# Moving the output weights' low half and the ternary weights to GpSimd, with new opening and closing order lists

## The chip, the cores and the metric

The kernel runs on one core of a Trainium2 chip. The metric is the device time of one execution, in microseconds (us). The core has a matrix engine (TensorE, PE), a vector engine (VectorE, DVE), an activation engine (ScalarE, ACT), a general engine (GpSimd, POOL) and a queue that issues transfers (SyncE, SP). Each runs its own instruction list in order and waits for the others through semaphores.

## The reference, cut to what matters

Gated cross attention over a context, then a quantised feed-forward block with ternary weights. There are 32 batches of 112 queries and 375 context rows, model width 256, 16 heads of 64.

```python
# x (32,112,256), ctx (32,375,256); weights in f32
q = layernorm(layernorm(x)) @ Wq ; k, v = split(layernorm(ctx) @ Wkv)
q = (q * (1 + scale) + shift) ; attn = softmax(q k^T / 8) ; out = (attn v) @ Wout
x = x + tanh(g_xattn) * out
def bitlinear(x, w, b):                     # w: one of 3 values times a scale
    scale = 1.0 / clip(mean(abs(w)), 1e-5)
    wq = clip(round(w * scale), -1, 1) / scale
    return act_quant(rmsnorm(x)) @ wq.T + b
x = x + tanh(g_ffn) * bitlinear(gelu(bitlinear(layernorm(x), w1, b1)), w2, b2)
```

## The kernel before

**Precision.** Operands of the attention part are held as two f16 tensors, a high half and the rest (low half), and every product is three f16 matmuls (high with high, high with low, low with high; lines 844 to 846). The four weight matrices are split once in the opening: ScalarE scales by 64 and rounds to f16 (`split_hi`, line 521), VectorE subtracts to get the low half (`split_lo`, line 650). The feed-forward weights become ternary once: VectorE sums their absolute values (steps AS0, AS1, line 662), TensorE adds them up (SUM), VectorE turns that into a scale (WM), ScalarE multiplies and rounds (RW0, RW1, line 526), and VectorE subtracts the rounding constant and clips (`ternary`, steps TN0 and TN1, lines 675 and 677), two passes over 128x2048 elements for each matrix.

**Steps.** The work is cut into named steps for a batch b. Z0, Z1 and ZX on TensorE transpose the normalised context and queries; ScalarE applies the layer norm weights (ZF0, ZF1, ZXF), GpSimd splits into halves (ZS0, ZS1, ZXS; VectorE does ZS1 of batch 0). K0 to K7 make the keys, Q0 and Q1 the queries, V00 to V12 the values; ScalarE takes each result's high half (KH, VH; QF for the queries, which GpSimd splits in QS0, QS1), VectorE its low half (KL, VL). For each pair of heads p: scores Sp on TensorE, maximum Mp on VectorE, exponentials Ep on ScalarE, high half PHp (ScalarE for even p, VectorE for odd), low half PLp on GpSimd (line 448), a transposing transfer Tp issued by SyncE (line 367), product Ap with the values on TensorE. N0 to N3 normalise, OO0/OO1 transpose the result, OH/OT split it. WO is the output projection for a tile of 128 rows; then the feed-forward of the tile: X1, XST, SC1, XR, XQ, XD (or XT), XTE, F0/F1, HE0/HE1, GE, SQ, HMX, RM2, SC2, HR, HQ, HD (or HT), HTE, F2, YE, ST. SC2 waits for RM2's result, which rests on SQ; HMX only needs GE. LNA on GpSimd and LNW on ScalarE normalise the next batch's inputs; LNW also has to be over before SyncE may load the batch after.

**Order.** Each engine's order is a list written out by hand: `FIRST` is the opening (from the first instruction to about the third batch's values), `ORDER` is repeated for the batches in the middle, `LAST` is the closing (from the last keys of batch 30 on). Number pairs such as ("K7", 0) are step and batch; K7 of batch 1 is written K7' below. Results of TensorE go to three PSUM banks in turn, in the order of the PE list, so a job waits until the job three places before it has been read out. An exponential step E waits for the PL two pairs before it (two buffers). The tensor `stage` holds all weights in f32; later the attention output (`ot`) and the feed-forward's hidden rows lie over it. So ScalarE's first OH0 waits for the low half of the output weights (`lo_split[3]`), TensorE's first F0 waits for `tern_ready[0]`, and ScalarE's first GE for `tern_ready[1]`; those first uses are in the fourth round or later.

In the opening ScalarE's list before is LNW, WKH0, ZF1, ZF0, WQH, WKH1, KH1, WVH, KH0, KH2, ZXF, WOH, KH4, KH3, LNW' and so on; WOH (the high half of the output weights) waits for their transfer, and everything behind it, LNW' too, waits with it.

Of the kernel before, what the change touches and what calls it, by code (L numbers as in the profile page):

```python
# [1007 lines left out]
```

## Time and profile before

| | us |
|---|---|
| median of 3 runs | 1119.94 (1119.65 to 1120.71) |
| the profiled execution, its own time | 1121.15 |
| its span, first to last instruction | 1119.3 |
| TensorE busy | 1068.0 (95%) |
| VectorE busy | 946.4 (85%) |
| ScalarE busy | 970.7 (87%) |
| GpSimd busy | 772.1 (69%) |

Busy time is a sum of instruction durations. In a timeline row the first number is the start, the second the duration, and the brackets say how long the engine had been idle and what released it. A stretch table gives for each engine the busy time with the number of instructions, then TensorE's granted clock (1.00 is 2.4 GHz, 0.50 is 1.2 GHz), the share of the transfer engines and their rate. Of the span, some 98 us are the opening, the last hundred or so are the closing list, and the rest is the middle.

### The profile page before, as it was taken

What the parts mean: (1) busy time and instruction counts of PE and PEld (TensorE: products, weight loads), DVE (VectorE), ACT (ScalarE), POOL (GpSimd) and SP (SyncE); (2) the same over time, 40 slices, a digit from 0 to 9 for tenths busy, and PEclk for the clock granted to TensorE, in tenths of its full rate; (3) what the DMA queues carried; (4) which work ended last, traced back from release to release, by engine and by line L of the source; (5) the groups of instructions that cost most, each with busy time, mean ns of one, the idle gap of its engine ahead of it and who ended that gap; (6) DMA issues with size and microseconds to landing.
All of it is one profiled execution on the core that took longest, in us unless ns stands there. A gap on an engine that the chain in (4) does not pass through costs nothing.

```text
span 1119.3 us, 32134 instructions
## 1 busy us (share of the span) xinstructions
PE 1068.0 (95%) x11910; PEld 733.5 (66%) x11910; DVE 946.4 (85%) x2112; ACT 970.7 (87%) x1865; POOL 772.1 (69%) x837
## 2 busy tenths in 40 slices
PE   3999999999999999999999999999999999999994
PEld 2566767666766766776766676776666676666662
DVE  5897788988888888888898878898888888888884
ACT  5788799999999799999999979999999988999762
POOL 3566676777667678767677766777766767777552
PEclk9899999999999999999999999999999999999996
DMA  8456667757667865687775575775667686654550
GB/s 272 86 109 107 101 106 122 123 97 126 115 114 118 133 104 101 123 115 110 134 119 99 120 118 99 122 127 104 115 119 120 109 137 112 97 124 106 112 114 24
DMA packets 408153, 129.08 MB, mean 115 GB/s; under 512 B 389792, under 2 KB 402848, under 8 KB 408000
## 3 DMA queue, kind: packets, MB, share of 16 engines
q1 hardware_dynamic: 408000, 127.03, 64.1%
q8 instruction: 98, 1.61, 0.6%
q14 instruction: 55, 0.45, 0.1%
HBM read 26.71 MB, written 3.67 MB: 27 GB/s over the span
## 4 chain that ended last, share of the span: by engine, by line
PE 78%; ACT 9%; DMA 5%; issue 3%; DVE 2%; POOL 1%; POOLq 0%; DVEq 0%; SPq 0%; ACTq 0%
PE work L844 16%; PE work L846 16%; PE work L845 16%; PE ps_s L863 11%; DMA pt<-pn 4%; PE ps_o L844 3%; PE ps_o L846 3%; PE ps_o L845 3%; PE work L927 3%; ACT prob L608 2%; ACT q_f L574 2%; ACT L608 2%; PE work L956 2%; PE work L918 2%; PE work L965 2%
## 5 line engine op out<-in xcount | busy, mean ns | idle before, releaser
L448 POOL TENSOR_TENSOR pn<-prob,pn 112x750 f16<-112x750 f32 x256 | 400.2, 1569 | 117.5 <-ACT pn L618 97.8
L608 ACT ACTIVATE prob<-ps_s,neg_max 112x375 f32<-112x375 f32 x512 | 265.1, 573 | 10.5 <-DVE neg_max L759 7.5
L759 DVE TENSOR_REDUCE neg_max<-ps_s 112x2 f32<-112x750 f32 x256 | 237.6, 929 | 21.6 <-PE ps_s L863 21.5
L844 PE MATMUL ps_o<-v_h,pt 128*128 128x65 f16 (+1 forms) x1536 | 166.5, 194 | 9.1 <-DMA pt<-pn 7.6
L844 PE MATMUL work<-z,wkv_h 128*128 128x375 f16 x512 | 168.4, 329 | 2.7 <-POOL z L469 2.5
L681 DVE SCALAR_TENSOR_TENSOR k_l<-work,k_h 128x375 f16<-128x375 f32 x256 | 136.4, 541 | 38.4 <-ACT k_h L530 38.3
L530 ACT ACTIVATE k_h<-work 128x375 f16<-128x375 f32 x256 | 121.4, 488 | 53.4 <-PE work L846 48.6
L846 PE MATMUL work<-z,wkv_l 128*128 128x375 f16 x512 | 167.2, 327 | 0.0
L845 PE MATMUL work<-z,wkv_h 128*128 128x375 f16 x512 | 166.8, 326 | 0.0
L845 PE MATMUL ps_o<-v_l,pt 128*128 128x65 f16 (+1 forms) x1536 | 166.3, 192 | 0.0
L846 PE MATMUL ps_o<-v_h,pt 128*128 128x65 f16 (+1 forms) x1536 | 166.3, 193 | 0.0
L844 PEld LDWEIGHTS ps_o<-v_h,pt 128*128 128x128 f16 (+1 forms) x1536 | 143.4, 97 | 22.5 <-DMA pt<-pn 10.4
L845 PEld LDWEIGHTS ps_o<-v_l,pt 128*128 128x128 f16 (+1 forms) x1536 | 142.6, 98 | 9.5
L844 PE MATMUL work<-wkv_h,z 128*128 128x512 f16 (+1 forms) x384 | 146.8, 382 | 1.2 <-DVE k_l L681 1.2
L846 PE MATMUL work<-wkv_h,z 128*128 128x512 f16 (+1 forms) x384 | 145.5, 379 | 0.0
L845 PE MATMUL work<-wkv_l,z 128*128 128x512 f16 (+1 forms) x384 | 145.4, 379 | 0.0
L846 PEld LDWEIGHTS ps_o<-v_h,pt 128*128 128x128 f16 (+1 forms) x1536 | 142.5, 97 | 0.0
L681 DVE SCALAR_TENSOR_TENSOR v_l<-work,v_h 128x512 f16<-128x512 f32 (+1 forms) x192 | 128.3, 681 | 7.1 <-ACT v_h L530 6.6
L530 ACT ACTIVATE v_h<-work 128x512 f16<-128x512 f32 (+1 forms) x192 | 115.3, 601 | 11.4 <-PE work L846 9.5
L618 ACT ACTIVATE pn<-prob 112x750 f16<-112x750 f32 x128 | 107.8, 842 | 0.1
L574 ACT ACTIVATE q_f<-work,side_add,side_mul 128x112 f32<-128x112 f32 x256 | 93.9, 466 | 2.9 <-PE work L846 2.8
L863 PE MATMUL ps_s<-k_h,q_h 64*112 64x375 f16 x512 | 88.7, 343 | 2.2 <-ACT prob L608 1.8
(135 smaller groups left out, 2723.5 us busy)
## 6 DMA issues: line engine op xcount, KB each, us to landing
ctx_in<-in_ctx SPq DMA_DIRECT2D x32, 375.0 KB
pt<-pn SPq DMA_TRANSPOSE x256, 3.5
x_in<-in_x SPq DMA_DIRECT2D x32, 112.0 KB, 3.8
x_res<-in_x SPq DMA_DIRECT2D x28, 128.0 KB, 5.0
out<-y SPq DMA_DIRECT2D x28, 128.0 KB, 2.0
stage<-in_wkv SPq DMA_DIRECT2D x2, 1024.0 KB, 9.3
stage<-in_w SPq DMA_DIRECT2D x2, 1024.0 KB, 13.1
stage<-in_wq SPq DMA_DIRECT2D x1, 1024.0 KB, 8.2
```

Of the source, the lines that this page charges most:

```text
L448: g.tensor_tensor(buf[:, 1, :, 0:SK], prob[:, p % 2], buf[:, 0, :, 0:SK], ALU.subtract).then_inc(p_lo, 1)
L530: a.activation(dst, src, ACT.Identity, scale=1.0 / W_SCALE).then_inc(hi_done, 1)
L574: i = a.activation(q_f[:, c, :], work[:, BANK[job], m * SQ:(m + 1) * SQ], ACT.Identity, bias=add, scale=mul)
L608: i = a.activation(prob[:, p % 2, h, :], ps_s[0:SQ, 2 * (p % 2) + h, 0:SK], ACT.Exp, bias=neg_max[:, 2 * (p % 2) + h:2 * (p % 2) + h + 1])
L618: a.activation(pn[g % PBUF][:, 0, :, 0:SK], prob[:, p % 2], ACT.Identity).then_inc(p_hi_act, 1)
L681: v.scalar_tensor_tensor(out=dst, in0=src, scalar=1.0 / W_SCALE, in1=hi_part, op0=ALU.mult, op1=ALU.subtract).then_inc(evacuated[BANK[job] ...
L759: v.tensor_reduce(neg_max[:, 2 * (p % 2):2 * (p % 2) + 2], ps_s[0:SQ, 2 * (p % 2):2 * (p % 2) + 2, 0:SK], X, ALU.max, negate=True).then_in ...
L844: t_.matmul(dst, sh, mh, start=(n == 0), stop=False)
L845: t_.matmul(dst, sh, ml, start=False, stop=False)
L846: i = t_.matmul(dst, sl, mh, start=False, stop=(n == len(pairs) - 1))
L863: i = t_.matmul(ps_s[0:SQ, 2 * (p % 2) + h, 0:SK], q[r, p, :], k[r, p, :], start=(n == 0), stop=(n == 2))
L927: i = t_.transpose(w[:, m * SQ:(m + 1) * SQ], attn[:, c * P:(c + 1) * P], ident[0:SQ, 0:SQ])
```

## The change

`ORDER`, which governs the middle, is not touched. Three steps move from VectorE's opening list to GpSimd's: WOL (low half of the output weights), TN0 and TN1 (the ternary weights). All `FIRST` and `LAST` lists are permuted. The steps are otherwise the same ones.

```diff
+            def split_output_weights():
+                pool.wait_ge(hi_split[3], 1)
+                g.tensor_scalar(wout_f, wout_f, W_SCALE, 0.0, ALU.mult, ALU.add)
+                pool.drain()
+                g.tensor_tensor(wout_l[:], wout_f, wout_h[:], ALU.subtract).then_inc(lo_split[3], 1)
+
+            def ternary(n):
+                w = (w1_f, w2_f)[n]
+                pool.wait_ge(tern_rounded[n], 1)
+                g.tensor_scalar(w, w, -ROUND, 1.0, ALU.add, ALU.min)
+                pool.drain()
+                g.tensor_scalar((w1_t, w2_t)[n][:], w, -1.0, 1.0, ALU.max, ALU.min).then_inc(tern_ready[n], 1)
...
-            def ternary(n):
-                w = (w1_f, w2_f)[n]
-                dve.wait_ge(tern_rounded[n], 1)
-                v.tensor_scalar(w, w, ROUND, 1.0, ALU.subtract, ALU.min)
-                dve.drain()
-                v.tensor_scalar((w1_t, w2_t)[n][:], w, -1.0, None, ALU.max).then_inc(tern_ready[n], 1)
...
-                if name == "WOL":
-                    split_lo(3, wout_f.rearrange("p (a k) n -> p a (k n)", a=2), wout_h[:].rearrange("p (a k) n -> p a (k n)", a=2),
-                             wout_l[:].rearrange("p (a k) n -> p a (k n)", a=2))
```

The opening lists, their start (PE to the first values; ScalarE, VectorE, GpSimd and SyncE as far):

```diff
 FIRST["PE"]
-    ("Z1", 0), ("Z0", 0), ("K1", 0), ("K0", 0), ("K2", 0), ("ZX", 0), ("K4", 0), ("K3", 0),
-    ("Q0", 0), ("Z0", 1), ("K7", 0), ("K5", 0), ("K6", 0), ("Z1", 1), ("S0", 0), ("S1", 0),
+    ("Z0", 0), ("Z1", 0), ("ZX", 0), ("K0", 0), ("K1", 0), ("K2", 0), ("Q0", 0), ("K4", 0),
+    ("K7", 0), ("S0", 0), ("K3", 0), ("Z1", 1), ("Z0", 1), ("S1", 0), ("S2", 0), ("K5", 0),
 FIRST["ACT"]
-    ("LNW", 0), ("WKH0", 0), ("ZF1", 0), ("ZF0", 0), ("WQH", 0), ("WKH1", 0), ("KH1", 0), ("WVH", 0),
-    ("KH0", 0), ("KH2", 0), ("ZXF", 0), ("WOH", 0), ("KH4", 0), ("KH3", 0), ("LNW", 1), ("QF0", 0),
+    ("WKH0", 0), ("LNW", 0), ("WKH1", 0), ("ZF0", 0), ("ZF1", 0), ("WQH", 0), ("ZXF", 0), ("KH0", 0),
+    ("KH1", 0), ("WVH", 0), ("KH2", 0), ("QF0", 0), ("KH4", 0), ("KH7", 0), ("WOH", 0), ("LNW", 1),
 FIRST["POOL"]
-    ("LNA", 0), ("ZS0", 0), ("ZXS", 0), ("LNA", 1), ("SD", 0), ("QS0", 0), ("ZS1", 1), ("ZS0", 1),
-    ("PL0", 0), ("PL1", 0), ("QS1", 0), ("PL2", 0), ("LNA", 2), ("PL3", 0), ("PL4", 0), ("GT", 0),
+    ("LNA", 0), ("ZS0", 0), ("SD", 0), ("ZXS", 0), ("QS0", 0), ("LNA", 1), ("WOL", 0), ("ZS0", 1),
+    ("PL0", 0), ("ZS1", 1), ("PL1", 0), ("QS1", 0), ("LNA", 2), ("PL2", 0), ("ZXS", 1), ("PL3", 0),
...
+    ("PL0", 1), ("PL1", 1), ("PL2", 1), ("QS1", 1), ("ZXS", 2), ("LNA", 3), ("PL3", 1), ("TN1", 0),
+    ("PL4", 1), ("TN0", 0), ("PL5", 1), ("QS0", 2), ("PL6", 1), ("ZS1", 3), ("PL7", 1), ("ZS0", 3),
 FIRST["SP"]
-    ("LX", 1), ("LD", 1), ("LW", 0), ("LD", 2), ("LX", 2), ("T0", 0), ("T1", 0), ("T2", 0),
+    ("LX", 1), ("LD", 1), ("LW", 0), ("RS", 1), ("LD", 2), ("LX", 2), ("T0", 0), ("T1", 0),
```

The closing lists, their ends:

```diff
 LAST["PE"]
-    ("A2", 31), ("A3", 31), ("WO", 30), ("F2", 28), ("A4", 31), ("A5", 31), ("A6", 31), ("A7", 31),
-    ("XT", 30), ("OO0", 31), ("OO1", 31), ("F0", 30), ("F1", 30), ("WO", 31), ("F2", 29), ("XT", 31),
+    ("WO", 30), ("F2", 28), ("A2", 31), ("A3", 31), ("A4", 31), ("A5", 31), ("OO0", 31), ("A6", 31),
+    ("A7", 31), ("XT", 30), ("OO1", 31), ("F1", 30), ("F0", 30), ("WO", 31), ("F2", 29), ("XT", 31),
 LAST["ACT"]
-    ("VH01", 31), ("VH02", 31), ("HR", 28), ("OH0", 30), ("PH4", 31), ("OH1", 30), ("E5", 31), ("VH10", 31),
-    ("VH11", 31), ("E6", 31), ("PH6", 31), ("E7", 31), ("VH12", 31), ("GE", 29), ("SQ", 29), ("XR", 30),
+    ("E4", 31), ("PH4", 31), ("VH02", 31), ("OH0", 30), ("E5", 31), ("KH7", 31), ("GE", 29), ("VH10", 31),
+    ("OH1", 30), ("E6", 31), ("VH12", 31), ("PH6", 31), ("VH11", 31), ("E7", 31), ("SQ", 29), ("OH0", 31),
 LAST["DVE"]
-    ("HE0", 31), ("HTE", 30), ("YE", 30), ("HMX", 31), ("SC2", 31), ("HTE", 31), ("YE", 31),
+    ("HE0", 31), ("HTE", 30), ("HMX", 31), ("YE", 30), ("SC2", 31), ("HTE", 31), ("YE", 31),
```

## Rows read from the trace of the kernel before

**Rows 1.** Stretch table, one round of the middle: busy by engine, clock, transfers.
```profile
157.10:190.50 33.40, 33.33 (x380) 23.21 (x378) 29.20 (x69) 30.81 (x60) 25.24 (x27) 1.00 0.65 113
```
**Rows 2.** Timeline of TensorE in the opening.
```profile
17.33 0.50 PE L844 MATMUL work<-z,wkv_h 128*128 128x375 f16 x1 [2.54 <-POOL z L469]
...
22.82 0.32 PE L844 MATMUL work<-z,wkv_h 128*128 128x375 f16 x1
...
22.98 0.32 PE L845 MATMUL work<-z,wkv_h 128*128 128x375 f16 x1
...
30.40 0.86 PE L918 MATMUL work<-ident,ctx_n 125*128 125x125 f32 x3 [3.74 <-ACT x_n L599]
```
**Rows 3.** Stretch table around the opening's wait.
```profile
28.00:30.00 2.00, 0.00 (x0) 0.00 (x0) 2.00 (x3) 2.00 (x5) 0.22 (x1) 0.78 0.47 173
...
30.00:40.00 10.00, 9.60 (x46) 5.46 (x47) 6.21 (x9) 4.71 (x12) 3.73 (x6) 0.70 0.22 66
```
**Rows 4.** Timeline of ScalarE in the opening.
```profile
13.07 1.04 ACT L521 ACTIVATE wkv_h<-stage 128x1024 f16<-128x1024 f32 x1
...
25.64 1.91 ACT L521 ACTIVATE wout_h<-stage 128x2048 f16<-128x2048 f32 x1 [1.66 <-DMA stage<-in_wout]
```
**Rows 5.** The chain that ended last, one pair's scores.
```profile
36.81 1.10 PE ps_s L863 x12
```
**Rows 6.** Groups by form on VectorE: the passes that leave it.
```profile
L675 DVE TENSOR_SCALAR stage<-stage 128x2048 f32<-128x2048 f32 x2 | 2.8, 1375 | 0.0
...
L677 DVE TENSOR_SCALAR w_t<-stage 128x2048 f16<-128x2048 f32 x2 | 2.6, 1323 | 0.2
...
L650 DVE SCALAR_TENSOR_TENSOR wout_l<-stage,wout_h 128x1024 f16<-128x1024 f32 x2 | 2.3, 1214 | 0.0
```
**Rows 7.** Groups by form on GpSimd: the nearest operations to those that arrive.
```profile
L448 POOL TENSOR_TENSOR pn<-prob,pn 112x750 f16<-112x750 f32 x256 | 400.2, 1569 | 117.5 <-ACT pn L618 97.8 <-DVE pn L766 19.5
...
L510 POOL TENSOR_SCALAR stage<-stage 128x1024 f16<-128x1024 f32 x28 | 37.6, 1342 | 16.7 <-ACT stage L637 16.7
...
L462 POOL TENSOR_TENSOR zx<-zxf,zx 128x224 f16<-128x224 f32 x32 | 19.6, 612 | 4.6
...
L497 POOL TENSOR_SCALAR xq<-xr 128x256 f16<-128x256 f32 x28 | 11.5, 412 | 6.0 <-ACT xr L621 5.9
```
**Rows 8.** Stretch table, late opening (columns as in Rows 1).
```profile
80.00:90.00 10.00, 9.65 (x108) 6.18 (x105) 7.97 (x21) 9.15 (x19) 6.96 (x7) 1.00 0.77 110
90.00:100.00 10.00, 8.60 (x97) 5.36 (x95) 6.79 (x14) 6.14 (x14) 5.53 (x6) 1.00 0.67 115
100.00:110.00 10.00, 9.97 (x131) 6.87 (x131) 9.73 (x16) 8.54 (x19) 8.37 (x8) 1.00 0.71 129
```
**Rows 9.** Waits from 78 to 95 us: total, times, longest.
```profile
PE ps_o L844 <- DMA pt<-pn: 1.4, 1, 1.4
...
PE ps_s L863 <- ACT prob L608: 0.8, 1, 0.8
```
**Rows 10.** VectorE's high-half casts: duration min/median/max in ns.
```profile
L766 DVE CAST pn<-prob x128: 535/543/1964, 43.7 to 1079.9; 112x750 f16<-112x750 f32 x128
```
**Rows 11.** Timeline of the closing.
```profile
1087.16 0.20 PE L844 MATMUL ps_o<-v_h,pt 128*128 128x65 f16 x1 [0.75 <-DMA pt<-pn]
...
1091.53 0.27 PE L844 MATMUL work<-wout_h,stage 128*128 128x256 f16 x1
...
1102.26 1.05 POOL L510 TENSOR_SCALAR stage<-stage 128x1024 f16<-128x1024 f32 x1 [3.21 <-ACT stage L637]
...
1107.34 0.48 DVE L832 SCALAR_TENSOR_TENSOR y<-work,deq2t,stage 128x256 f32<-128x256 f32 x1 [2.15 <-PE work L965]
1107.74 1.21 DVE L824 TENSOR_REDUCE amax<-stage 128x1 f32<-128x1024 f32 x1
```
**Rows 12.** Stretch table, TensorE's longest idle stretch before the last attention step.
```profile
1032.00:1042.00 10.00, 7.67 (x76) 4.38 (x75) 9.93 (x15) 7.06 (x14) 7.99 (x8) 1.00 0.58 138
```
**Rows 13.** Timeline of ScalarE: a table load between GE and E.
```profile
1059.85 1.28 ACT L608 ACT_TABLE_LOAD   x1
```

More of the change, by code:

```diff
@@ L475, in layernorm_scales @@
                 g.tensor_tensor(ln_nb[0:TP, :], ln_nm[0:TP, :], ln_rs[0:TP, :], ALU.mult).then_inc(ln_ready, 1)
+            def split_output_weights():
[9 more added lines that the diff above has]
+                g.tensor_scalar((w1_t, w2_t)[n][:], w, -1.0, 1.0, ALU.max, ALU.min).then_inc(tern_ready[n], 1)
             def step(name, b):
+                if name == "WOL":
+                    split_output_weights()
+                if name in ("TN0", "TN1"):
+                    ternary(int(name[2]))
                 if name == "SD":
@@ L745, in step @@
                     weight_means()
-                if name in ("TN0", "TN1"):
-                    ternary(int(name[2]))
                 if name in ("VL00", "VL01", "VL02", "VL10", "VL11", "VL12"):
```

145 rows, old and new, of the table CAST_ACT are left out of this document.

## The prediction

> **What bounds the kernel now.** I read the page first, then tables of stretches, then waits and timelines of the two ends. The reader is to see three regimes. In the middle TensorE is busy 33.33 of 33.40 us in a round [rows 1]; `ORDER` is not touched, so that part keeps its time, and since TensorE is its bound, what the opening saves or loses arrives whole at its end. In the opening TensorE is also the engine with most to do, but it stops: it starts its first keys at 17.33 and later idles 3.74 us until 30.40, for LNW' [rows 2]. ScalarE could not do LNW' earlier because it had WOH in front, which began at 25.64 when its transfer landed [rows 4]. During that idle the granted clock fell to 0.50: it is 0.78 over the last two idle microseconds and 0.70 over the following ten [rows 3]. In the closing TensorE first idles a little (7.67 of 10 us busy in the worst stretch [rows 12]) and then, from the last attention step on, everything is one chain of small steps.
>
> The sum is made on the profiled execution, 1121.15 us with a span of 1119.3; the median of the runs is 1119.94, 1.2 lower. I take the savings off the median.
>
> **The opening, start.** WKH0 goes ahead of LNW. It took 1.04 us at 13.07 [rows 4], after LNW; ahead of it, it lies in the time in which ScalarE waits for the statistics. What covers it is the landing of the first key weights; if they land late, LNW starts up to 1.04 later. WKH1 then fits while TensorE transposes, and Z0 before Z1 lets the slower splitter, GpSimd, begin first. I take 0.5 for the earlier first key, between 0 and 1.04.
>
> **The opening, the long wait.** WOH is still in front of LNW', and the transfer it waits for is issued as before. So I expect Z1' at about 30.2, almost the old 30.40. What changes is what is done by then: in the new PE list K7 and S0 come before Z1', in the old one behind Z0'. A key job is six matmuls at 0.16 us apart [rows 2], 0.96; a pair's scores take 1.10 [rows 5]. With the 0.2 from the earlier Z1' that is 2.2 us saved. S0 waits for QS0, and LNA' is behind QS0 on GpSimd, so the old single wait of 3.74 us becomes two: some 1.5 us ahead of S0 and some 1.5 ahead of Z1', with 2 us of work between them.
>
> **The clock.** A mean of 0.70 over ten microseconds is 6 us at half [rows 3]; the first 0.4 of them were idle, so 5.6 us ran work that takes 2.8 at full clock: 2.8 us lost. I take it as saved, since no new idle piece is as long as the one that brought the clock down; the other end is nothing saved. This is the least certain term.
>
> **WOL on GpSimd.** On VectorE it is two instructions of 1.21 us, 2.4 in all [rows 6]. Those lie in VectorE's slack in the long wait, so removing them saves nothing. On GpSimd the subtraction has no row of its size: 224 elements take 0.61 and 750 take 1.57 [rows 7], 1.82 ns an element, so 2048 take 1.57 + 1298 x 1.82 ns = 3.9 us. The scaling pass comes from 256 elements in 0.41 [rows 7] and 1024 in 1.05 [rows 11], giving 1.9; with the mean 1.34 of the 1024-element passes [rows 7] it is 2.6. WOL is thus 5.8 to 6.5, from 28 to 34 us. Queued behind it are ZS0', PL0, ZS1'. The new PE list has S1, S2, K5, K6, V02, V00, Q1, V01, ZX' and S3 (some 10 us) before K0', the first that needs ZS0' and ZS1', so cost 0; if it took twice as long it would cost 1 to 2 us.
>
> **TN0 and TN1 on GpSimd.** On VectorE they took 2.8 + 2.6 = 5.4 us [rows 6] in one piece in front of a maximum; behind that is the 0.8 us for which TensorE waited on an exponential [rows 9]. On GpSimd they are four passes, 1.9 to 2.6 each: 7.6 to 10.3 us. The order is PL3', TN1, PL4', TN0, PL5'; behind them wait E6' and E7', T4' and T5', A4' and A5', then QS0 and the splits for batch 3. From 80 to 110 us GpSimd was busy 6.96 + 5.53 + 8.37 = 20.9 of 30 us [rows 8], so there are 9.1 us free: just enough for the low price, not for the high one. PL4' gets some 2 us later, PL5' some 2.5. A4' was already 1.4 us late for its transposed operand [rows 9] but is now at the end of the list, 2.2 us of work later. I take 0.8 saved, and 1.6 lost by later splits and products: net -0.8, between +2 and -4.
>
> All in the opening: 2.2 + 2.8 - 0.8 = 4.2.
>
> **The rule that speaks against it.** VectorE's cast has a median of 543 ns but took 1964 once [rows 10], 1.4 us more, about what one of GpSimd's low-half steps lasts (1.57 [rows 7]). The Trainium skill, page "SBUF — State Buffer", section "Who interferes with whom", says that the two engines share one port pair which the first holds for its whole instruction. The trace agrees as far as that one row goes. By that rule each 1.9 to 3.9 us pass on GpSimd can hold up VectorE's next cast for that long; it is the slower rival below.
>
> **RS and the other moves.** The first residual load goes to the opening's start on SyncE's queue, behind the late weights and ahead of LD of batch 2, which waits for LNW' anyway: nothing.
>
> **The closing.** (a) HMX of the last tile took 1.21 us at 1107.74, behind YE of the tile before, which had waited for its F2 until 1107.34 [rows 11]. In the new list HMX is ahead of YE, in VectorE's idle 2.15 us before it; SC2 follows 1.2 us sooner and all behind it. (b) OO0 of batch 31 moves ahead of A6, out of the stretch between A7 and the last WO at 1091.53 [rows 11]: 0.4. (c) GE of batch 29 now lies between exponentials: two more table loads of 1.28 [rows 13]. One hides in ScalarE's idle time at the end, the other is in front of E6 and E7, whose results the last A7 waits for (it waited 0.75 [rows 11]); -0.4, between 0 and -1.3. (d) TensorE's idle time before A7, 2.3 of it in one stretch [rows 12]; other lists give back half, +1.2, between -1.5 and +3.5. Sum 2.4.
>
> **Rivals.** *The clock falls all the same* (20%): the two waits are too near each other. Then 6.6 - 2.8 = 3.8 saved, 1116.1. For it: TensorE is busy only two of five microseconds there. *The ternary passes crowd GpSimd* (13%): at 10.3 us against 9.1 free, every PL late in the opening moves an A; worth 4 us of the 6.6, 1117.3. *More is won* (9%): the waits of the opening's later part go entirely and so does the closing's idle time, another 4: 1109.3. *The new lists do not do it* (9%): landing times set the opening's pace, other waits take the closing's; 1119.9. *Slower* (9%): while GpSimd holds the port for its long passes, casts PH1 and PH3 and the small scalings on VectorE stand still, and with them the maxima queued behind. Its place is WOL and the two TN, six long passes, 13.4 us at the low price; if two thirds of that reached TensorE, 9 us, it would eat the 6.6 and more: 1122.3. It decides from the point where half of those passes, 6.7 us, reach TensorE. Against it: maxima and most evacuations read PSUM, and the middle lives with 256 passes of 1.57 [rows 7] while TensorE stays full [rows 1].
>
> **How the numbers follow.** The forecast, 4.2 + 2.4 = 6.6 saved, 40%: 1119.94 - 6.6 = 1113.3. The range takes in the case of more won and those of the fallen clock and of the crowding and leaves out the last two: 1109.0 to 1118.5. About 0.2% (2.2 us, so 1117.7) is what a measurement can tell from no change. Faster by more: 40 + 20 + 9 and two thirds of 13, 0.78. Within: 9 and the rest of 13, 0.13. Slower: 0.09.
>
> **What would show it.** First key at about 16.9; idle before Z1' about 1.5 us, not 3.74, and the clock at 1.00 from 30 to 40; the middle's rounds unchanged at 33.4; four GpSimd passes of 1.9 to 2.6 near 80 to 95 us with TensorE not idle behind them; HMX ahead of YE and SC2 right behind YE at the end; from A7 to the end 1.6 us less. Wrong would be: a longer wait for LNW', the clock at 0.50 after it, VectorE casts of 2 to 4 us beside the long passes, or TensorE waiting for PL4' and PL5'.

## The result

The changed kernel takes 1131.95 us (median of 5 runs, 1130.10 to 1133.43), the kernel before beside it 1120.71 (5 runs, 1119.65 to 1120.81): a ratio of 1.0101, interval 1.0087 to 1.0115. It is slower by 11 us; the forecast was 6.6 us faster. The profiled execution took 1130.10 with a span of 1128.0, against 1121.15 and 1119.3 before.

Line numbers moved: the pair product is L850 to L852 instead of L844 to L846, the low-half step of attention (PL) L449, the scores L869, LayerNorm's output L616, the exponential L626. The new steps are L480 and L482 (WOL) and L487 and L489 (TN0, TN1). The groups by form on GpSimd, changed kernel (busy us, mean ns of one, then the idle time before):

```profile
L489 POOL TENSOR_SCALAR w_t<-stage 128x2048 f16<-128x2048 f32 x2 | 14.3, 7128 | 0.3 <-issue 0.3
L487 POOL TENSOR_SCALAR stage<-stage 128x2048 f32<-128x2048 f32 x2 | 14.2, 7097 | 0.0
L482 POOL TENSOR_TENSOR wout_l<-stage,wout_h 128x2048 f16<-128x2048 f32 x1 | 4.1, 4092 | 0.1
L480 POOL TENSOR_SCALAR stage<-stage 128x2048 f32<-128x2048 f32 x1 | 1.9, 1900 | 0.0
```

WOL came out as priced: 1.9 and 4.1 us against 1.9 and 3.9. The two ternary steps did not: L480 is a pass over 128x2048 elements in 1.90 us, L487 one over the same shape and types in 7.10. Four of them are 28.5 us, where the prediction had 7.6 to 10.3 and GpSimd had 9.1 free [rows 8].

What the 28.5 us do is seen in three views of the changed kernel. GpSimd's timeline around them:

```profile
76.86 1.56 POOL L449 TENSOR_TENSOR pn<-prob,pn 112x750 f16<-112x750 f32 x1
78.39 7.12 POOL L487 TENSOR_SCALAR stage<-stage 128x2048 f32<-128x2048 f32 x1
85.65 7.18 POOL L489 TENSOR_SCALAR w_t<-stage 128x2048 f16<-128x2048 f32 x1 [0.15 <-issue]
92.82 1.55 POOL L449 TENSOR_TENSOR pn<-prob,pn 112x750 f16<-112x750 f32 x1
94.34 7.08 POOL L487 TENSOR_SCALAR stage<-stage 128x2048 f32<-128x2048 f32 x1
101.57 7.08 POOL L489 TENSOR_SCALAR w_t<-stage 128x2048 f16<-128x2048 f32 x1 [0.15 <-issue]
108.62 1.56 POOL L449 TENSOR_TENSOR pn<-prob,pn 112x750 f16<-112x750 f32 x1
...
110.83 1.03 POOL L457 TENSOR_TENSOR q_l<-q_f,q_h 128x448 f16<-128x448 f32 x1
```

The waits from 85 to 120 us (us in total, times, longest):

```profile
ACT prob L626 <- POOL pn L449: 19.4, 2, 12.0
...
PE ps_s L869 <- POOL q_l L457: 8.4, 1, 8.4
...
PE ps_o L850 <- DMA pt<-pn: 7.2, 1, 7.2
```

And the stretch tables over it and in parts of it, and one round of the middle in the last row, columns as in [rows 1]:

```profile
85.00:120.00 35.00, 19.43 (x182) 11.94 (x182) 12.30 (x22) 10.91 (x25) 34.00 (x15) 0.71 0.23 47
94.00:101.00 7.00, 3.47 (x24) 2.28 (x25) 2.50 (x5) 3.85 (x9) 7.00 (x2) 0.50 0.22 49
112.00:120.00 8.00, 7.99 (x72) 4.92 (x74) 5.33 (x9) 4.49 (x11) 7.45 (x7) 0.70 0.57 110
157.10:190.50 33.40, 33.25 (x373) 22.79 (x372) 29.53 (x71) 31.59 (x62) 24.35 (x27) 1.00 0.65 109
```

Read together: PL3' ends at 78.4, and PL4' starts at 92.8 because TN1 is in between. Two things wait for PL4'. Its own transposing transfer does, and behind it TensorE's A4', 7.2 us. So does the exponential two pairs later, E6', whose buffer comes free then: ScalarE stands for 7.4 us. TN0 then holds PL5' until 108.6, and ScalarE stands for another 12.0, 19.4 in all, with VectorE's casts behind it. QS0 of the next batch, queued behind PL5' on GpSimd, makes TensorE wait 8.4 us for `q_l`. TensorE works 19.4 of 35 us where it used to work more than nine tenths [rows 8]. Its granted clock is 0.50 (1.2 GHz) from 94 to 101, the end of the wait of 7.2 us and what follows it, and it is down again behind the wait of 8.4: 0.70 from 112 to 120. The middle is the old one: 33.25 busy of 33.40 (last row) against 33.33 [rows 1].

One marker divides the span into its first 440 us or so, the opening with some rounds of the middle, and the rest: LayerNorm's output for the same batch of the middle, on ScalarE, first in the changed kernel, then in the one before:

```profile
456.69 1.58 ACT L616 ACTIVATE ctx_n<-ctx_in,ln_nb,ln_rs 125x256 f32<-125x256 f32 x3
```
```profile
442.40 1.58 ACT L598 ACTIVATE ctx_n<-ctx_in,ln_nb,ln_rs 125x256 f32<-125x256 f32 x3
```

Up to there the changed kernel is 14.3 us behind. From the marker to the end it needs 1128.0 - 456.69 = 671.3, the old one 676.9: it gets back 5.6. Together 8.7, the difference of the spans.

### The profile page after: what moved, and what is told of

Read it like the earlier page. It is cut to its first block, busy times and chain, and to the rows that moved or that the text cites. A ratio compares the mean times of both kernels' runs of the same rounds, so it can differ in the third digit from the quotient of the medians.

```text
span 1128.0 us, 32136 instructions
## 1 busy us (share of the span) xinstructions
PE 1068.8 (95%) x11910; PEld 734.3 (65%) x11910; DVE 938.3 (83%) x2106; ACT 972.7 (86%) x1867; POOL 808.1 (72%) x843
## 4 chain that ended last, share of the span: by engine, by line
PE 75%; ACT 8%; POOL 5%; DMA 5%; issue 4%; POOLq 2%; DVE 2%; DVEq 0%; ACTq 0%
PE work L850 16%; PE work L852 15%; PE work L851 15%; PE ps_s L869 11%; DMA pt<-pn 5%; PE ps_o L850 3%; PE ps_o L852 3%; PE ps_o L851 3%; PE work L933 2%; ACT prob L626 2%; ACT q_f L592 2%; ACT L626 2%; PE work L962 2%; PE work L924 2%; PE work L971 2%
## 5 line engine op out<-in xcount | busy, mean ns | idle before, releaser
L449 POOL TENSOR_TENSOR pn<-prob,pn 112x750 f16<-112x750 f32 x256 | 400.1, 1569 | 106.5 <-ACT pn L636 95.3
L626 ACT ACTIVATE prob<-ps_s,neg_max 112x375 f32<-112x375 f32 x512 | 265.3, 574 | 27.8 <-POOL pn L449 20.0
L850 PE MATMUL ps_o<-v_h,pt 128*128 128x65 f16 (+1 forms) x1536 | 167.0, 194 | 13.9 <-DMA pt<-pn 12.1
L850 PE MATMUL work<-z,wkv_h 128*128 128x375 f16 x512 | 167.3, 327 | 3.1 <-issue 2.2
L852 PE MATMUL ps_o<-v_h,pt 128*128 128x65 f16 (+1 forms) x1536 | 166.7, 193 | 0.0
L852 PE MATMUL work<-z,wkv_l 128*128 128x375 f16 x512 | 166.4, 325 | 0.0
L850 PEld LDWEIGHTS ps_o<-v_h,pt 128*128 128x128 f16 (+1 forms) x1536 | 143.6, 97 | 27.7 <-DMA pt<-pn 14.9
L851 PEld LDWEIGHTS ps_o<-v_l,pt 128*128 128x128 f16 (+1 forms) x1536 | 142.8, 98 | 10.4 <-issue 0.3
L850 PE MATMUL work<-wkv_h,z 128*128 128x512 f16 (+1 forms) x384 | 148.4, 386 | 0.5 <-DVE v_l L692 0.4
L852 PE MATMUL work<-wkv_h,z 128*128 128x512 f16 (+1 forms) x384 | 146.8, 382 | 0.0
L852 PEld LDWEIGHTS ps_o<-v_h,pt 128*128 128x128 f16 (+1 forms) x1536 | 142.7, 97 | 0.0
L869 PE MATMUL ps_s<-k_h,q_h 64*112 64x375 f16 x512 | 89.3, 345 | 11.2 <-POOL q_l L457 10.9
```

Of the source, the lines that this page charges most:

```text
L449: g.tensor_tensor(buf[:, 1, :, 0:SK], prob[:, p % 2], buf[:, 0, :, 0:SK], ALU.subtract).then_inc(p_lo, 1)
L626: i = a.activation(prob[:, p % 2, h, :], ps_s[0:SQ, 2 * (p % 2) + h, 0:SK], ACT.Exp, bias=neg_max[:, 2 * (p % 2) + h:2 * (p % 2) + h + 1])
L850: t_.matmul(dst, sh, mh, start=(n == 0), stop=False)
L851: t_.matmul(dst, sh, ml, start=False, stop=False)
L852: i = t_.matmul(dst, sl, mh, start=False, stop=(n == len(pairs) - 1))
L869: i = t_.matmul(ps_s[0:SQ, 2 * (p % 2) + h, 0:SK], q[r, p, :], k[r, p, :], start=(n == 0), stop=(n == 2))
```

## Why 7.1 us: the passes priced one by one

Two explanations of a 7.1 us pass were open. Either the operation itself is dear on GpSimd (both ternary passes have a minimum in them, WOL's has none), or it is slowed by VectorE's work at the same time, by the port that the prediction's slower rival was about. *pass_prices* appends eleven passes to the old kernel's GpSimd, behind the last store, when no other engine works. It ran once; only its rows are used. In short:

```diff
+            pool.wait_ge(y_stored, 16 * NT)
+            g.tensor_scalar(d, s, 1.0, 1.0, ALU.add, ALU.mult)
+            g.tensor_scalar(d, s, 1.0, 1.0, ALU.add, ALU.min)
+            g.tensor_scalar(d, s, -1.0, 1.0, ALU.max, ALU.min)
+            g.tensor_scalar(d, s, 1.0, 1.0, ALU.min, ALU.mult)
+            g.tensor_scalar(d, s, 1.0, 0.0, ALU.max, ALU.add)
+            g.tensor_scalar(h, s, -1.0, 1.0, ALU.max, ALU.min)
+            g.tensor_scalar(h, s, 1.0, 1.0, ALU.add, ALU.mult)
+            g.tensor_scalar(d[:, 0], s[:, 0], -1.0, 1.0, ALU.max, ALU.min)
+            g.tensor_scalar(d[:, 0, 0:HALF], s[:, 0, 0:HALF], -1.0, 1.0, ALU.max, ALU.min)
+            g.tensor_scalar(d, s, 1.0, 1.0, ALU.add, ALU.max)
+            g.tensor_tensor(d, s, s, ALU.subtract)
```

> The kernel before, with eleven passes over weights added on GpSimd after the last store, when VectorE is idle. Theory A: 128x2048 f32 with add and multiply 1.9 us; every form with a minimum or maximum 7.1 us, into f32 or f16; 1024 elements 3.6 us, 512 elements 1.9 us; subtraction of two tensors 3.9 to 4.1. Theory C (contention): all single-tensor forms take 1.9 us here. The total time is longer by the sum of the passes, some 50 us, and says nothing.

GpSimd's timeline of that kernel, the passes in the order of the diff (start, duration):

```profile
1118.55 1.90 POOL L519 TENSOR_SCALAR stage<-stage 128x2048 f32<-128x2048 f32 x1 [6.41 <-DMA out<-y]
1120.60 7.10 POOL L521 TENSOR_SCALAR stage<-stage 128x2048 f32<-128x2048 f32 x1
1127.85 7.08 POOL L523 TENSOR_SCALAR stage<-stage 128x2048 f32<-128x2048 f32 x1 [0.15 <-issue]
1135.09 7.09 POOL L525 TENSOR_SCALAR stage<-stage 128x2048 f32<-128x2048 f32 x1 [0.15 <-issue]
1142.33 7.09 POOL L527 TENSOR_SCALAR stage<-stage 128x2048 f32<-128x2048 f32 x1 [0.15 <-issue]
1149.58 7.08 POOL L529 TENSOR_SCALAR w_t<-stage 128x2048 f16<-128x2048 f32 x1 [0.15 <-issue]
1156.81 1.90 POOL L531 TENSOR_SCALAR w_t<-stage 128x2048 f16<-128x2048 f32 x1 [0.15 <-issue]
1158.86 3.62 POOL L533 TENSOR_SCALAR stage<-stage 128x1024 f32<-128x1024 f32 x1 [0.15 <-issue]
1162.63 1.92 POOL L535 TENSOR_SCALAR stage<-stage 128x512 f32<-128x512 f32 x1 [0.15 <-issue]
1164.70 7.09 POOL L537 TENSOR_SCALAR stage<-stage 128x2048 f32<-128x2048 f32 x1 [0.15 <-issue]
1171.94 3.60 POOL L539 TENSOR_TENSOR stage<-stage 128x2048 f32<-128x2048 f32 x1
```

Add with multiply takes 1.90 us, with f32 (L519) or f16 results (L531). Every pass that has a minimum or a maximum, as first or second operation, takes 7.08 to 7.10, whichever result it writes. It is a price for each element: 3.62 us for 1024 and 1.92 for 512, so (7.08 - 1.92) / 1536 = 3.4 ns an element, against 1.90 us / 2048 = 0.9. VectorE is idle here, so contention isn't the cause: 7.1 us is what these forms cost. The subtraction of two tensors (L539) took 3.60, less than the 3.9 to 4.1 expected.

The Trainium skill, page "GPSIMD Engine Reference", section 4.1, lists add, mul and max together and says of operations with one input that GpSimd is "roughly line-rate". The 1.90 us pass may be read so; the 7.08 us pass with a maximum and a minimum contradicts it.

## Is that the whole loss?

*tn_cheap_forms* keeps the changed kernel's lists and its four passes, but with the operations that take 1.9 us. It leaves out the clipping of the weights. The experiments ran in three groups, each with the kernel before beside it (medians 1120.45, 1120.90 and 1121.29); differences "against before" are taken within a group.

```diff
-                g.tensor_scalar(w, w, -ROUND, 1.0, ALU.add, ALU.min)
+                g.tensor_scalar(w, w, -ROUND, 1.0, ALU.add, ALU.mult)
                 pool.drain()
-                g.tensor_scalar((w1_t, w2_t)[n][:], w, -1.0, 1.0, ALU.max, ALU.min).then_inc(tern_ready[n], 1)
+                g.tensor_scalar((w1_t, w2_t)[n][:], w, 1.0, 0.0, ALU.mult, ALU.add).then_inc(tern_ready[n], 1)
```

> The changed kernel with the ternary passes on GpSimd at their places and sizes, but with add and multiply in place of add and minimum, and multiply and add in place of maximum and minimum. The clipping to three values is left out of the computation by that. Theory A (a minimum or maximum in the pass makes it slow): each pass takes 1.9 us as the scaling pass of WOL does, four 7.6 us, and TensorE's waits of 7.2 and 8.4 us nearly go: 1109 to 1115. Theory C (the passes are long because the port is held by VectorE, or because of their place in the list): they still take over 4 us each and the time stays at 1125 or more.

Measured: 1111.75 us (1110.72 to 1113.44), ratio 0.9922 (0.9906 to 0.9938), 20.2 us below the changed kernel and 8.7 below the one before (1120.45 beside it). Its groups on GpSimd, and its stretch table for the same 35 us:

```profile
L489 POOL TENSOR_SCALAR w_t<-stage 128x2048 f16<-128x2048 f32 x2 | 3.9, 1948 | 0.3 <-issue 0.3
L487 POOL TENSOR_SCALAR stage<-stage 128x2048 f32<-128x2048 f32 x2 | 3.8, 1897 | 0.0
```
```profile
85.00:120.00 35.00, 32.97 (x376) 22.73 (x375) 28.64 (x53) 25.70 (x54) 26.61 (x24) 1.00 0.60 97
```

TensorE is busy 32.97 us in place of 19.43, at full clock. The 13.5 us of difference is idle time. The rest is the clock. In the changed kernel TensorE worked at half clock for 3.5 us from 94 to 101, for 2.2 more until 103.2 by its timeline, and from 112 to 120 for 8 x 0.30 x 2 = 4.8: 10.5 us, of which 5.2 are lost. Together that is 18.7. The passes began at 78.39 in the changed kernel and at 80.44 in this one, and the markers are at 456.69 and 440.32, so 16.4 + 2.05 = 18.4 us were lost in between: the sum closes within 0.3.

*before_tn_on_gpsimd* does that one part alone: old kernel, old lists, TN1 behind PL3' and TN0 behind PL4' on GpSimd.

```diff
-    ("BB", 3), ("M1", 1), ("VL00", 1), ("N2", 0), ("VL01", 1), ("TN0", 0), ("VL02", 1), ("KL0", 2),
-    ("TN1", 0), ("M2", 1), ("PH1", 1), ("OT0", 0), ("M3", 1),
+    ("BB", 3), ("M1", 1), ("VL00", 1), ("N2", 0), ("VL01", 1), ("VL02", 1), ("KL0", 2),
+    ("M2", 1), ("PH1", 1), ("OT0", 0), ("M3", 1),
...
-    ("QS1", 1), ("PL1", 1), ("PL2", 1), ("LNA", 3), ("ZXS", 2), ("PL3", 1), ("PL4", 1), ("QS0", 2),
+    ("QS1", 1), ("PL1", 1), ("PL2", 1), ("LNA", 3), ("ZXS", 2), ("PL3", 1), ("TN1", 0), ("PL4", 1), ("TN0", 0), ("QS0", 2),
```

> The kernel before with its old lists, TN0 and TN1 alone moved to GpSimd, at the places behind PL3 and PL4 of batch 1 as in the change. Theory A: 28.6 us of passes against 9.1 us free on GpSimd from 80 to 110 us, so 16 to 20 us lost: 1136 to 1141. Theory B (lists): within 3 us of before, 1118 to 1124.

Measured: 1141.56 (1140.78 to 1141.68), ratio 1.0185 (1.0170 to 1.0200), 21.1 us slower than before, 0.6 above the 1136 to 1141 expected. Its waits from 78 to 125 us have the same two on TensorE, 10.7 us and 6.7:

```profile
PE ps_o L844 <- DMA pt<-pn: 10.7, 1, 10.7
...
PE ps_s L863 <- POOL q_l L456: 6.7, 1, 6.7
```

So the dear forms cost 20.2 us in the new lists, the whole move 21.1 in the old ones, and the new lists with cheap passes in them save 8.7.

## Where the ternary steps should go

*tn_on_vector* is the changed kernel with TN0 and TN1 on VectorE again, TN0 behind KL0 of batch 2 and TN1 at the end of the opening list.

```diff
 FIRST["DVE"]
-    ("VL00", 1), ("M2", 1), ("VL02", 1), ("PH1", 1), ("KL0", 2), ("N2", 0), ("VL01", 1), ("BB", 3),
-    ("M3", 1), ("OT0", 0),
+    ("VL00", 1), ("M2", 1), ("VL02", 1), ("PH1", 1), ("KL0", 2), ("TN0", 0), ("N2", 0), ("VL01", 1), ("BB", 3),
+    ("M3", 1), ("OT0", 0), ("TN1", 0),
 FIRST["POOL"]
-    ("PL0", 1), ("PL1", 1), ("PL2", 1), ("QS1", 1), ("ZXS", 2), ("LNA", 3), ("PL3", 1), ("TN1", 0),
-    ("PL4", 1), ("TN0", 0), ("PL5", 1), ("QS0", 2), ("PL6", 1), ("ZS1", 3), ("PL7", 1), ("ZS0", 3),
+    ("PL0", 1), ("PL1", 1), ("PL2", 1), ("QS1", 1), ("ZXS", 2), ("LNA", 3), ("PL3", 1),
+    ("PL4", 1), ("PL5", 1), ("QS0", 2), ("PL6", 1), ("ZS1", 3), ("PL7", 1), ("ZS0", 3),
```

> The changed kernel with TN0 and TN1 back on VectorE (in its new opening list behind KL0 of batch 2 and at the list's end); the new lists and WOL on GpSimd stay. Theory A (the four ternary passes of 7.1 us on GpSimd are the whole loss): the opening's lead of 6.4 us, read at the layer norm of batch 3, survives less about 1 us for the 5.5 us of passes on VectorE, and the closing keeps its 5.6: 1120.7 - 5 - 5 = about 1110, between 1107 and 1114. Theory B (the new lists themselves, or the held port, cost the time): 1120 or more.

Measured: 1122.98 (1120.81 to 1124.36), ratio 1.0022 (1.0011 to 1.0032). This is a miss: 1107 to 1114 was expected, and by the number alone it would speak for Theory B. Its VectorE timeline and TensorE's two longest waits from 15 to 160 us show why:

```profile
68.93 2.36 DVE L684 TENSOR_SCALAR stage<-stage 128x2048 f32<-128x2048 f32 x1
...
82.17 1.23 DVE L684 TENSOR_SCALAR stage<-stage 128x2048 f32<-128x2048 f32 x1 [4.17 <-ACT stage L535]
```
```profile
PE ps_o L850 <- issue: 4.0, 1, 4.0
PE ps_o L850 <- DVE attn L699: 3.5, 1, 3.5
```

There are two losses. TN1 stood at the head of VectorE's queue for 4.17 us, waiting for ScalarE's rounding of the second weights, with KL1, N3 and the rest behind it; TensorE stood for 4.0 us until N3's normalisation (`attn`) ended at 85.74. I had put the step where VectorE had room, not where its input was ready. And TN0, in front of N2, took 2.36 and 2.42 us where TN1 took 1.23 and 1.23: GpSimd ran PL steps and a cast beside it, from 68.6 to 74.2. TensorE waited 3.5 us for N2. Its clock fell behind both waits, to a mean of 0.83 from 70 to 80 and from 80 to 90. *ternary_on_vector_placed* repeats the run with TN0 behind M1' and TN1 behind M4'. Against the changed kernel, with GpSimd's list as in *tn_on_vector*:

```diff
-    ("KL7", 1), ("KL5", 1), ("WM", 0), ("KL6", 1), ("M0", 1), ("N1", 0), ("BA", 3), ("M1", 1),
+    ("KL7", 1), ("KL5", 1), ("WM", 0), ("KL6", 1), ("M0", 1), ("N1", 0), ("BA", 3), ("M1", 1), ("TN0", 0),
...
-    ("M3", 1), ("OT0", 0),
+    ("M3", 1), ("OT0", 0), ("KL1", 2), ("N3", 0), ("BS", 3), ("PH3", 1), ("VL10", 1), ("VL11", 1), ("M4", 1), ("TN1", 0),
```

> The changed kernel with both ternary steps wholly on VectorE, as in tn_on_vector, but TN0 behind M1 and TN1 behind M4 of batch 1, where the rounded weights are there already. Theory: tn_on_vector lost its time because its TN1 stood 4.2 us waiting for ScalarE's rounding ahead of steps that TensorE needed, so here 1114 to 1117. Rival (VectorE has no 5.4 us free in the new lists at all): 1120 or more.

Measured: 1115.09 (1114.11 to 1116.00), ratio 0.9952 (0.9938 to 0.9967), within the 1114 to 1117 expected and 7.9 us below *tn_on_vector* (8.7, each taken against its own kernel before): the same two steps on the same engine, placed otherwise. That speaks against Theory B as well. How the 7.9 divide between TN0's place and TN1's was not run.

*split_passes* divides each step by what each engine does cheaply: VectorE clips to ROUND ± 1 in one pass (max, min), GpSimd subtracts ROUND in one pass (add, mult). CL0 stands behind M1' and CL1 behind M4' on VectorE, TN0 behind PL3' and TN1 behind PL4' on GpSimd.

```diff
+            def clip(n):
+                w = (w1_f, w2_f)[n]
+                dve.wait_ge(tern_rounded[n], 1)
+                v.tensor_scalar(w, w, ROUND - 1.0, ROUND + 1.0, ALU.max, ALU.min).then_inc(tern_clipped[n], 1)
...
             def ternary(n):
                 w = (w1_f, w2_f)[n]
-                pool.wait_ge(tern_rounded[n], 1)
-                g.tensor_scalar(w, w, -ROUND, 1.0, ALU.add, ALU.min)
-                pool.drain()
-                g.tensor_scalar((w1_t, w2_t)[n][:], w, -1.0, 1.0, ALU.max, ALU.min).then_inc(tern_ready[n], 1)
+                pool.wait_ge(tern_clipped[n], 1)
+                g.tensor_scalar((w1_t, w2_t)[n][:], w, -ROUND, 1.0, ALU.add, ALU.mult).then_inc(tern_ready[n], 1)
```

> The changed kernel with the ternary step divided by what each engine does cheaply: VectorE clips the rounded weights to the rounding constant plus or minus 1 in one pass of 1.2 us (behind M1 and behind M4 of batch 1), GpSimd subtracts the constant with an add-and-multiply pass of 1.9 us at the change's places. Everything is computed. Theory A (the form of the pass on GpSimd is the loss, the rest of the change is a gain): as the run with cheap forms, 1111.75, or up to 2 us more for VectorE's 2.4 us: 1111 to 1114. Theory B (VectorE has no room there either): 1117 or more.

Measured: 1114.80 (1113.93 to 1115.14), ratio 0.9942 (0.9930 to 0.9955), 0.8 above the range expected. Its timelines of VectorE (the second clip), GpSimd and TensorE show a small loss that remained:

```profile
81.70 2.49 DVE L691 TENSOR_SCALAR stage<-stage 128x2048 f32<-128x2048 f32 x1
```
```profile
81.21 1.90 POOL L487 TENSOR_SCALAR w_t<-stage 128x2048 f16<-128x2048 f32 x1
```
```profile
84.70 0.43 PE L855 MATMUL work<-wkv_h,z 128*119 128x512 f16 x1 [1.92 <-DVE k_l L695]
```

The first clip, at 66.40, takes 1.22 us. The second starts while GpSimd's pass runs (81.21 to 83.11) and takes 2.49: the remaining 1.41 us of that pass and its own 1.22 nearly add up. KL behind it is late and TensorE waits 1.92 us. *split_passes_later* takes CL1 and TN1 a few steps back. Against *split_passes*:

```diff
-    ("M3", 1), ("OT0", 0), ("KL1", 2), ("N3", 0), ("BS", 3), ("PH3", 1), ("VL10", 1), ("VL11", 1), ("M4", 1), ("CL1", 0),
+    ("M3", 1), ("OT0", 0), ("KL1", 2), ("N3", 0), ("BS", 3), ("PH3", 1), ("VL10", 1), ("VL11", 1), ("M4", 1), ("KL2", 2), ("M5", 1), ("KL3", 2), ("OT1", 0), ("VL12", 1), ("N0", 1), ("CL1", 0),
...
-    ("PL4", 1), ("TN1", 0), ("PL5", 1), ("QS0", 2), ("PL6", 1), ("ZS1", 3), ("PL7", 1), ("ZS0", 3),
+    ("PL4", 1), ("PL5", 1), ("TN1", 0), ("QS0", 2), ("PL6", 1), ("ZS1", 3), ("PL7", 1), ("ZS0", 3),
```

> The run with divided passes, with VectorE's second clip moved from behind M4 to behind N0 of batch 1 and GpSimd's second subtraction behind PL5. In the divided run that clip took 2.49 us beside GpSimd's first subtraction (1.22 alone) and TensorE waited 1.92 us for a low half behind it. Theory: the 3 us between the divided run (1114.8) and the cheap forms (1111.75) are this wait: 1112 to 1113.5. Rival (VectorE's work itself, not its place): no change, 1114.8.

Measured: 1112.82 (1111.73 to 1114.85), ratio 0.9935 (0.9919 to 0.9952). Its second clip, on VectorE, runs undisturbed, and no wait of TensorE from 65 to 95 us is longer than 0.5:

```profile
84.22 1.22 DVE L691 TENSOR_SCALAR stage<-stage 128x2048 f32<-128x2048 f32 x1
```

The wait went. The median is 2.0 lower than that of *split_passes* (2.4 against before), but the two intervals overlap, so the gain itself isn't shown.

## The other terms of the sum, one at a time

*old_opening_new_closing* is the old kernel with the new closing lists; *new_opening_old_closing* is *split_passes* with the old ones; *wol_on_vector* is *split_passes* with WOL on VectorE. The edits, in short (TensorE's closing list stands for all five; the second and third edit are against *split_passes*):

```diff
 LAST["PE"]
-    ("Q0", 30), ("K4", 30), ("Z1", 31), ("A2", 29), ("A3", 29), ("K6", 30), ("S0", 30), ("K7", 30),
+    ("Q0", 30), ("Z1", 31), ("K7", 30), ("A2", 29), ("Q1", 30), ("K4", 30), ("S0", 30), ("ZX", 31),
...
```

> The kernel before with the new closing lists alone. The profile of the change has the closing 5.6 us shorter: 1114 to 1116. Rival: the 5.6 came from how the new opening left the middle, not from the lists: 1119 to 1121.

```diff
 LAST["PE"]
-    ("Q0", 30), ("Z1", 31), ("K7", 30), ("A2", 29), ("Q1", 30), ("K4", 30), ("S0", 30), ("ZX", 31),
+    ("Q0", 30), ("K4", 30), ("Z1", 31), ("A2", 29), ("A3", 29), ("K6", 30), ("S0", 30), ("K7", 30),
...
```

> The run with divided passes, with the old closing lists. The two ends add up: the difference to before is what the divided run saves less what the closing alone saves, 1115 to 1117. Rival (an interplay): outside that.

```diff
 FIRST["DVE"]
-    ("M0", 0), ("AS0", 0), ("KL3", 0), ("AS1", 0), ("KL5", 0), ("M1", 0), ("KL6", 0), ("VL02", 0),
+    ("WOL", 0), ("M0", 0), ("AS0", 0), ("KL3", 0), ("AS1", 0), ("KL5", 0), ("M1", 0), ("KL6", 0), ("VL02", 0),
 FIRST["POOL"]
-    ("LNA", 0), ("ZS0", 0), ("SD", 0), ("ZXS", 0), ("QS0", 0), ("LNA", 1), ("WOL", 0), ("ZS0", 1),
+    ("LNA", 0), ("ZS0", 0), ("SD", 0), ("ZXS", 0), ("QS0", 0), ("LNA", 1), ("ZS0", 1),
```

> The run with divided passes, with WOL back on VectorE as its two instructions of 1.2 us, ahead of M0 of batch 0. The prediction's price for moving it is 0 because the jobs behind it on GpSimd have 10 us of cover: within 1.5 us of the run with divided passes. Rival: GpSimd gains room for batch 1's splits, 2 us or more faster.

| kernel | us (range) | ratio (interval) | against before, us |
|---|---|---|---|
| old_opening_new_closing | 1116.84 (1115.86 to 1118.18) | 0.9965 (0.9953 to 0.9978) | -4.1 |
| new_opening_old_closing | 1118.20 (1117.02 to 1118.46) | 0.9971 (0.9959 to 0.9983) | -2.7 |
| split_passes | 1114.80 (1113.93 to 1115.14) | 0.9942 (0.9930 to 0.9955) | -6.1 |
| wol_on_vector | 1114.84 (1113.82 to 1115.23) | 0.9943 (0.9929 to 0.9956) | -6.1 |

They ran beside one median of before, 1120.90. *old_opening_new_closing* lies 0.8 above its expected range and *new_opening_old_closing* 1.2 above, on the side that its expectation calls an interplay; but the two halves give 6.8 and both together 6.1, so they add up within the spread. Moving WOL changes nothing that the runs can tell, 0.04 us.

The last one goes for the opening's waits. In the changed kernel the first key, S0 and Z1' on TensorE, and LNW' on ScalarE, read:

```profile
17.56 0.47 PE L850 MATMUL work<-z,wkv_h 128*128 128x375 f16 x1 [2.18 <-issue]
...
28.39 0.56 PE L869 MATMUL ps_s<-k_h,q_h 64*112 64x375 f16 x2 [2.47 <-POOL q_l L457]
...
31.83 0.84 PE L924 MATMUL work<-ident,ctx_n 125*128 125x125 f32 x6 [0.25 <-ACT x_n L617]
```
```profile
29.61 1.58 ACT L616 ACTIVATE ctx_n<-ctx_in,ln_nb,ln_rs 125x256 f32<-125x256 f32 x3 [1.37 <-POOL ln_nb L476]
```

LNW' is late because LNA', its input on GpSimd, is queued behind QS0. *earlier_layer_norm* (the edit is against *split_passes_later*) puts LNA' ahead of QS0, LNW' ahead of WOH and K3 ahead of S0:

```diff
 FIRST["PE"]
-    ("K7", 0), ("S0", 0), ("K3", 0), ("Z1", 1), ("Z0", 1), ("S1", 0), ("S2", 0), ("K5", 0),
+    ("K7", 0), ("K3", 0), ("S0", 0), ("Z1", 1), ("Z0", 1), ("S1", 0), ("S2", 0), ("K5", 0),
 FIRST["ACT"]
-    ("KH1", 0), ("WVH", 0), ("KH2", 0), ("QF0", 0), ("KH4", 0), ("KH7", 0), ("WOH", 0), ("LNW", 1),
+    ("KH1", 0), ("WVH", 0), ("KH2", 0), ("QF0", 0), ("KH4", 0), ("KH7", 0), ("LNW", 1), ("WOH", 0),
 FIRST["POOL"]
-    ("LNA", 0), ("ZS0", 0), ("SD", 0), ("ZXS", 0), ("QS0", 0), ("LNA", 1), ("WOL", 0), ("ZS0", 1),
+    ("LNA", 0), ("ZS0", 0), ("SD", 0), ("ZXS", 0), ("LNA", 1), ("QS0", 0), ("WOL", 0), ("ZS0", 1),
```

> As split_passes_later, and the second batch's layer norm no longer behind other steps: LNA of batch 1 ahead of QS0 on GpSimd, LNW of batch 1 ahead of WOH on ScalarE, K3 ahead of S0 on TensorE. In the change's profile TensorE waited 2.47 us ahead of S0 and then about 2 us ahead of Z1 of batch 1, with the granted clock down between 27 and 36 us. Theory: the prediction's second wait is owed to LNA queued behind QS0, so Z1' comes at 29.5 and not at 31.8 and the clock stays up more: 2 to 5 us less, 1107.5 to 1111. Rival: the splits of batch 1 behind WOL become the bound, within 1 us of split_passes_later.

Measured: 1112.30 (1110.59 to 1113.54), ratio 0.9926 (0.9910 to 0.9942): the lowest but for *tn_cheap_forms*, yet only 0.5 below *split_passes_later*, which the runs can't tell from nothing, where 1107.5 to 1111 had been expected. Its stretch table and TensorE's timeline:

```profile
25.00:30.00 5.00, 3.77 (x28) 2.26 (x25) 3.45 (x5) 4.97 (x11) 3.07 (x3) 1.00 0.94 329
30.00:40.00 10.00, 8.42 (x68) 5.00 (x67) 9.78 (x11) 7.93 (x18) 8.85 (x6) 1.00 0.20 74
```
```profile
28.68 0.37 PE L874 MATMUL ps_s<-k_h,q_h 64*112 64x375 f16 x2 [1.23 <-POOL q_l L457]
```

The mechanism is as meant: the wait ahead of S0 is 1.23 instead of 2.47, Z1' begins at 29.3 (29.5 expected), and the clock stays at 1.00. But with a full clock TensorE runs into the next engine: it is busy 8.42 of the ten microseconds from 30 and waits 1.33 for an exponential at 32.11. In *split_passes_later* the same stretches have a lower clock and are fuller:

```profile
25.00:30.00 5.00, 2.53 (x14) 1.15 (x13) 3.77 (x5) 3.54 (x6) 4.12 (x5) 0.86 0.98 345
30.00:40.00 10.00, 9.62 (x74) 5.87 (x73) 9.26 (x11) 8.14 (x19) 9.56 (x7) 0.90 0.24 77
```

From 25 to 30 it issues 28 matmuls instead of 14, from 30 to 40 then 68 instead of 74, both times at full clock. What it gained there was largely lost again in small waits behind: from 40 to 160 us TensorE waits 2.1 us for transposed operands and 1.9 for GpSimd's splits of z, against 0.8 and 0.9 in *split_passes_later*. Which moved step makes them was not run.

## The prediction against the runs

- **TN0 and TN1 on GpSimd: the step that failed.** The text prices "four passes, 1.9 to 2.6 each" from the rows of L497 and L510 [rows 7] and their like in size. Those are passes without a minimum or maximum; the ones that arrived have it and take 7.1 each. The bound from both sides was made along the size of the operation alone, so the true value lay far outside, and "between +2 and -4" was too narrow by some 16 us. The comparison with "9.1 us free" was the right one: with 28.5 in it, it gives 19.4 us too much, and 20 to 21 were lost at the end, the fallen clock included. By the prediction's own order of work (PL3', TN1, PL4', TN0, PL5', and E6' and E7' behind) that could have been read off at once. One reading was off without effect: in the trace of before the two steps are not in one piece, TN0 runs from 70.3 to 72.8 and TN1 from 73.8 to 76.8, with two low-half steps in between.
- **The rivals.** *The ternary passes crowd GpSimd* (13%) named the mechanism and the place, but at 10.3 us and 4 lost. The slower rival put the loss on the port, and that is not the cause: *pass_prices* has 7.1 us with VectorE idle. The hold is real but small here. The changed kernel's cast beside L487, on VectorE's timeline, takes 2.31 us where 543 ns is the median [rows 10]:

```profile
83.60 2.31 DVE L772 CAST pn<-prob 112x750 f16<-112x750 f32 x1
```

  The Trainium skill, page "SBUF — State Buffer", section "Who interferes with whom", says that whoever issues first holds the shared pair for its whole instruction. The trace agrees with it on VectorE's side: the cast ended at 85.91, 0.4 us after GpSimd's pass (78.39 + 7.12 = 85.51), and the clip of 2.49 in *split_passes* at 84.19, 1.1 after the pass that ended at 83.11, each about its own length later (0.54 and 1.22). The same shows in TN0 of *tn_on_vector*, 4.8 us in place of 2.5, where it did reach TensorE.
- **WOL.** Right: 1.90 + 4.09 us, cost 0.0 by *wol_on_vector*.
- **The opening, start.** Wrong by its sign: the first key is at 17.56, not 16.9 (17.33 before [rows 2]). The transfer for WKH0 landed at 10.4, so LNW began after it, at 11.3 instead of 11.1, and the first key waited for VectorE's half of z, whose subtraction took 1.17 us and ended at 17.46. Small, 0.7 us.
- **The opening, the long wait.** The 3.74 us [rows 2] became 2.47 ahead of S0 and 0.25 ahead of Z1', where 1.5 and 1.5 were forecast; but Z1' came at 31.83, not 30.2, as LNA' is behind QS0. I had named that queue and not carried its time into Z1'. The reading of before was off in the same place: GpSimd's timeline there has the end of LNA' at 27.29 + 0.20 = 27.49, and LNW' began at 28.19, so WOH in front of it can have cost 0.7 at most. The rest of that wait was LNA' being late on GpSimd.

```profile
27.29 0.20 POOL L475 TENSOR_TENSOR ln_nb<-ln_nm,ln_rs 125x4 f32<-125x4 f32 x1
```

- **The clock.** Between the forecast and the rival *the clock falls all the same*, and nearer the rival. From 30 to 40 the changed kernel's stretch table shows 0.92 (below) where [rows 3] has 0.70. But part of its time at half clock lies before 30, where the mean over five microseconds is 0.81: 5 x 0.19 x 2 + 10 x 0.08 x 2 = 3.5 us at half, 1.7 lost at most. So at least 1.1 of the 2.8 was gained, and not all of it. The profiles of the seven kernels with these lists up to there fall into two kinds: 3.4 to 3.5 us at half between 25 and 40 (the changed kernel, *split_passes_later*, *ternary_on_vector_placed*) and 6.8 to 6.9, as much as before (*split_passes*, *tn_cheap_forms*, *tn_on_vector*, *new_opening_old_closing*). That is 1.7 us between kernels that are alike there, one profile each; what decides it stays open. Only *earlier_layer_norm*, with two waits of 1.23 and 1.33, shows 1.00 from 25 to 40.

```profile
30.00:40.00 10.00, 9.75 (x75) 5.76 (x73) 9.42 (x11) 8.25 (x19) 9.56 (x7) 0.92 0.22 73
```

- **The opening as a whole.** Forecast 4.2. With passes of 1.9 us it is 2.7 (*new_opening_old_closing*) to 4.6 (the 8.7 of *tn_cheap_forms* less the closing's 4.1).
- **The closing.** Forecast 2.4, measured 4.1 alone and 5.6 by the marker in the profiles. Not all of the 5.6 is the new lists': *new_opening_old_closing*, with the old ones, needs 1115.0 - 439.70 = 675.3 us behind the marker, 1.6 less than before. (a) Right: HMX is now ahead of YE, and SC2 starts 0.6 us after YE instead of 1.7 (1107.34 [rows 11] and 1109.03), 1.1 saved for 1.2. From the start of the last A7 to the end of the span it is 1128.0 - 1097.52 = 30.5 us against 1119.3 - 1087.16 = 32.1 [rows 11], 1.6 less, as said. (d) was too low: marker to A7 is 1097.52 - 456.69 = 640.8 against 1087.16 - 442.40 = 644.8, so 3.9 where (c) and (d) had 0.8. Which of the moves brought it was not run. VectorE's timeline shows HMX, YE and SC2:

```profile
1115.19 1.21 DVE L830 TENSOR_REDUCE amax<-stage 128x1 f32<-128x1024 f32 x1
1117.42 0.48 DVE L838 SCALAR_TENSOR_TENSOR y<-work,deq2t,stage 128x256 f32<-128x256 f32 x1 [1.02 <-PE work L971]
1118.01 0.21 DVE L729 TENSOR_SCALAR clip<-amax,g_rs 128x1 f32<-128x1 f32 x1
```

- **The sum without the ternary passes.** 6.6 forecast. With passes at the price assumed, the kernels that still clip measured 6.1 (*split_passes*) and 8.5 (*split_passes_later*), *tn_cheap_forms* 8.7. One price of a form that the trace of before doesn't hold turned it into 11 lost. The 9% for slower was too little for a term whose dearest input had no row of its own operation.

*split_passes_later* (1112.8) and *earlier_layer_norm* (1112.3) beat both kernels, by 8.5 and 9.0 us against before and by 19 to 20 against the changed one.

## What to carry to other kernels

Before a step changes its engine, look for a row of that engine with the same arithmetic functions, not only with the same size and type; where there is none, measure the form (here one run appended to the kernel's end settled it) or let the range hold several times the price. If only part of a step is dear on the new engine, divide the step. And place it where its input is ready: a step at the head of a queue holds all behind it, and one beside GpSimd's work took up to twice as long. The same two steps placed otherwise were worth some 8 us here.
